# A three-block transformer megakernel on one Trainium2 core: the mixer's decay sums repeated over the partitions by a DMA in place of selector matmuls

## The chip, the core and the metric

The kernel runs on one core of one Trainium2 chip. A core has five engines with queues of their own that work in order and meet in semaphores: TensorE (matmuls, PE in the profile; PEld is its loading of the stationary operand), VectorE (DVE), ScalarE (ACT), GpSimd (POOL) and SyncE (SP), which here issues nearly all DMAs. The metric is the device time of one execution in microseconds. It was 2147.99 us, the median of three runs (2144.83, 2147.99 and 2150.49).

## The reference, cut to what matters

The input is x, 4 batches of 256 rows of 512. Four blocks are added to it one after another: attention, a feed-forward with a row mask, a Mamba-2 mixer, and the feed-forward again. The change is in the mixer, which has 128 heads of 64 channels in 8 groups of 16 heads. With `cum` the running sum of dt times A over the rows of a head, it computes

```python
cum = jnp.cumsum(dA.reshape(b, nc, CS, H), axis=2)
Ldec = jnp.exp(cum[:, :, :, None, :] - cum[:, :, None, :, :])
Ldec = jnp.where(mask[None, None, :, :, None], Ldec, 0.0)
scores = jnp.einsum('bcihn,bcjhn->bcijh', Cc, Bc) * Ldec * dtc[:, :, None, :, :]
y_intra = jnp.einsum('bcijh,bcjhp->bcihp', scores, xc)
...
y = (y_intra + y_inter).reshape(b, l, H, P) + Dp[None, None, :, None] * x
...
g = y * jax.nn.silu(gate)
var = jnp.mean(gg * gg, axis=-1, keepdims=True)
g = (gg * jax.lax.rsqrt(var + EPS)).reshape(b, l, INTER) * norm_w
return g @ out_w.T
```

The reference goes in chunks with a state between them. The kernel computes the same sum in one piece: for every head a full lower triangle of exp(cum_i - cum_j) over the 256 rows of a batch.

## The kernel before

The four blocks run one after another, with a barrier between them. The mixer (`build_mixer`, line 982) takes from about 480 to 2085 us. It starts with a stage of its own for dt and the decay sums (lines 1020 to 1175): DVE computes dt and `cum` as [128 heads, 1024 rows] in fp32, then splits `cum` into three bf16 parts (lines 1132 to 1140), and SP writes each part to DRAM (`cum_parts`, line 1050). TensorE also transposes dt and `cum`, so that rows lie on partitions (`dt_rows`, `ncum_rows`).

Then come 8 groups (`over_groups`, line 1248: the first and the last written out, a loop over the six between), each with 8 pairs of heads, k = 0 to 7. The order on each engine is written out by hand in that engine's `body`. In pair k of group g:

- TensorE (line 1777) makes the two projections for the next pair (x and gate, `product`, 24 matmuls of 512 columns each: fp32 operands are split in a high and a low part, and `three_pass` adds three products), the output products of pairs done before (`out_rows`), and the pair's own y (`y_of_pair`, line 1742: 32 matmuls from `decay` and `x_dt`). `spread_cum` (line 1688) makes the decay sums of one head, one row of 1024 values, stand on all 128 partitions: two matmuls of a constant 0/1 tensor `sel` with `cum`, the group's three bf16 parts, into PSUM banks 2 and 3. It waits until ACT has made the exponentials of the head before (`exped`), since both heads use these banks.
- DVE (line 1595): `causal` takes the minimum of these banks with a mask into `decay` (L1542; a is 0 or 1, the head in the pair); the taps of the convolution (L1518); `mix` multiplies `decay` with the group's C.B product `cb` (L1551); the skip term after y (L1640). In pairs 2 and 3 it adds finished rows to x (L1584).
- ACT (line 1453): `exps` makes 12 exponentials of 128 columns a head, four of them (L1407) straight from banks 2 and 3 and eight in place in `decay` (L1412); between the two heads come the first tap of the convolution, the square, and `scale_wo` (line 1416), which waits for the output weight of this pair, scales it (L1423) and rounds it (L1425); after them the silu functions and `high` (L1434).
- POOL (line 1352): splits of the projection weights (L1308, L1310) and of the output weight (L1323), gating (`gate_pair`, L1333, and g_lo, L1338), sums of squares (L1344).
- SP (line 1279): per pair two loads of projection weights (`load_w`, L1271, each waits for a split three loads back on POOL) and one of the output weight (`load_wo`, L1276, into one of two buffers, waits for the split two pairs back). The weights loaded at pair k of SP's body are those of the projections for pair k+2; the output weight is the one of pair k.

The feed-forward blocks load, after 1 MB of weights, two rows that a DMA repeats over partitions (the cluster numbers over 64, the bias over 128). These are used in the rows below.

Of the kernel before, what the change touches and what calls it, by code (L numbers as in the profile page):

```python
# [15 lines left out]
F32 = mybir.dt.float32  # L16
# [7 lines left out]
P = 128  # L24
# [957 lines left out]
def build_mixer(nc, sh, ins):  # L982
    with ExitStack() as ctx:
# [7 lines left out]
        cum_parts = nc.dram_tensor("cum_parts", (3, MH, ROWS), BF16, kind="Internal").ap()  # L991
# [6 lines left out]
        sel = sb("sel", [3 * GHEADS, GHEADS, P], BF16)  # L998
# [21 lines left out]
        with ExitStack() as inner:  # L1020
            def isb(name, shape, dt=F32):
# [7 lines left out]
            parts = isb("parts", [MH, 3, ROWS], BF16)  # L1029

            made, w_in, c_in, w_done = sem("dt_made"), sem("dt_w_in"), sem("dt_c_in"), sem("dt_w_done")
            proj, step, ex, split, moved = (sem("dt_proj"), sem("dt_step"), sem("dt_exp"), sem("dt_split"),
                                            sem("dt_moved"))
            turned = sem("dt_turned")
            block = inner.enter_context(nc.Block())

            @block.sync
            def _(sp):
# [9 lines left out]
                for part in range(3):  # L1048
                    sp.wait_ge(split, (1, 3, 5)[part])
                    sp.dma_start(cum_parts[part, :, :], parts[:, part, :]).then_inc(moved, 16)  # L1050
                sp.wait_ge(moved, 3 * 16)

            @block.gpsimd
            def _(pool):
# [7 lines left out]
                pool.memset(sel[:, :, :], 0.0).then_inc(made, 1)  # L1062
# [3 lines left out]
                for part in range(3):  # L1066
                    pool.wait_ge(made, 2 + part)
                    pool.affine_select(out=sel[:, :, :], in_=sel[:, :, :], compare_op=ALU.not_equal, fill=1.0,
                                       base=-part * GHEADS, pattern=[[-1, GHEADS], [0, P]], channel_multiplier=1)\
                        .then_inc(made, 1)  # L1070
# [23 lines left out]
            def _(dve):  # L1094
# [32 lines left out]
                dve.wait_ge(made, 2)  # L1127
# [7 lines left out]
                dve.wait_ge(split, 2)  # L1135
                dve.tensor_copy(parts[:, 1, :], e[:, :]).then_inc(split, 1)
                dve.wait_ge(split, 3)
                dve.tensor_tensor(s1[:, :], e[:, :], parts[:, 1, :], ALU.subtract).then_inc(split, 1)
                dve.wait_ge(split, 4)
                dve.tensor_copy(parts[:, 2, :], s1[:, :]).then_inc(split, 1)  # L1140
# [8 lines left out]
            def _(pe):  # L1149
# [17 lines left out]
                STEPS = 17  # L1167
# [16 lines left out]
        cum = sb("cum", [3 * GHEADS, ROWS], BF16)  # L1184
# [15 lines left out]
        cum_arrived = sem("cum_arrived")  # L1200
# [3 lines left out]
        spread, exped, selected, mixed, y_done = (sem("spread"), sem("exped"), sem("selected"), sem("mixed"),  # L1204
                                                  sem("y_done"))
# [60 lines left out]
        def _(sp):  # L1266
# [11 lines left out]

            def body(g, first, last):

                at_least(sp, spread, GHEADS * g)
                for part in range(3):
# [385 lines left out]
        def _(pe):  # L1668
# [19 lines left out]
            def spread_cum(g, k, a, first):  # L1688

                head = GHEADS * g + 2 * k + a  # L1690
                if k == 0 and a == 0:
                    pe.wait_ge(cum_arrived, 3 * 16 * (g + 1))
                    if first:

                        pe.wait_ge(convolved, 12)
# [226 lines left out]
```

## Time and profile before

| | |
|---|---|
| median of the runs | 2147.99 us (2144.83 to 2150.49) |
| profiled execution | span 2145.0 us; the page gives no other time for it |
| PE busy | 1998.4 us, 93% |
| DVE busy | 1469.8 us, 69% |
| ACT busy | 1252.7 us, 58% |
| POOL busy | 1036.5 us, 48% |
| DMA moved | 70.50 MB, mean 33 GB/s |
| granted TensorE clock, mean | 0.957 |

Times in the profile are from the first instruction of the execution. Matmuls overlap, so the duration of one is longer than the step to the next. The timeline merges neighbours of one kind (xcount; the second column is then the time from the first's start to the last's end), and puts the idle time before an instruction, with what ended it, in brackets. The granted clock is 1.00 at 2.4 GHz and 0.50 at 1.2 GHz; in the mixer's loop from 541 to 2056 us it is 1.00 throughout.

### The profile page before, as it was taken

What the parts mean: (1) busy time and instruction counts of PE and PEld (TensorE: products, weight loads), DVE (VectorE), ACT (ScalarE), POOL (GpSimd) and SP (SyncE); (2) the same over time, 40 slices, a digit from 0 to 9 for tenths busy, and PEclk for the clock granted to TensorE, in tenths of its full rate; (3) what the DMA queues carried; (4) which work ended last, traced back from release to release, by engine and by line L of the source; (5) the groups of instructions that cost most, each with busy time, mean ns of one, the idle gap of its engine ahead of it and who ended that gap; (6) DMA issues with size and microseconds to landing.
All of it is one profiled execution on the core that took longest, in us unless ns stands there. A gap on an engine that the chain in (4) does not pass through costs nothing. (4 is left out here: it accounts for less than half of the span.)

```text
span 2145.0 us, 32211 instructions
## 1 busy us (share of the span) xinstructions
PE 1998.4 (93%) x10956; PEld 1533.1 (71%) x10956; DVE 1469.8 (69%) x2060; ACT 1252.7 (58%) x2621; POOL 1036.5 (48%) x841
## 2 busy tenths in 40 slices
PE   6989997758999999999999999999999999999977
PEld 4855775536777777777777777777777777777755
DVE  5466555676677786777768766876777677678756
ACT  3221332326675776667757766775777577666733
POOL 4001001534565566466645654665566466646535
PEclk9965998879999999999999999999999999999988
DMA  3000001001101111110111111111111111111002
GB/s 99 1 1 20 2 2 30 25 27 50 35 30 42 31 40 35 38 35 31 37 37 40 35 37 36 30 40 36 37 35 32 41 31 40 32 40 35 20 1 69
DMA packets 40720, 70.50 MB, mean 33 GB/s; under 512 B 7392, under 2 KB 7520, under 8 KB 40544
## 3 DMA queue, kind: packets, MB, share of 16 engines
q1 hardware_dynamic: 39584, 68.21, 10.5%
q8 instruction: 97, 1.59, 0.3%
q14 instruction: 79, 0.65, 0.1%
q10 hardware_dynamic: 960, 0.05, 0.0%
HBM read 65.34 MB, written 2.88 MB: 32 GB/s over the span
## 5 line engine op out<-in xcount | busy, mean ns | idle before, releaser
L143 PE MATMUL ps<-mix_xnT_hi,mix_w_hi 128*128 128x512 f32 x1152 | 461.8, 401 | 12.0 <-DVE mix_bT L1518 7.0
L145 PE MATMUL ps<-mix_xnT_hi,mix_w_lo 128*128 128x512 f32 x1152 | 455.1, 395 | 0.0
L144 PE MATMUL ps<-mix_xnT_lo,mix_w_hi 128*128 128x512 f32 x1152 | 454.9, 395 | 0.0
L1308 POOL TENSOR_TENSOR mix_w_hi<-mix_w_raw,mix_ones 128x512 fp32r<-128x512 f32 x141 | 178.0, 1263 | 470.0 <-PE ps L145 467.2
L1518 DVE SCALAR_TENSOR_TENSOR mix_xT<-ps,mix_cur,mix_xT 128x510 f32<-128x510 f32 x378 | 280.7, 746 | 108.4 <-ACT mix_xT L1384 99.4
L1412 ACT ACTIVATE mix_decay<-mix_decay,mix_cur_ncum 128x128 f32<-128x128 f32 x1024 | 353.1, 397 | 0.0
L143 PEld LDWEIGHTS ps<-mix_xnT_hi,mix_w_hi 128*128 128x128 f32 x1152 | 217.4, 189 | 63.9 <-issue 12.8
L1551 DVE TENSOR_TENSOR mix_decay<-mix_decay,mix_cb 128x1536 f32<-128x1536 f32 x128 | 242.1, 1897 | 21.8 <-ACT mix_decay L1412 21.2
L145 PEld LDWEIGHTS ps<-mix_xnT_hi,mix_w_lo 128*128 128x128 f32 x1152 | 217.3, 189 | 50.9
L1407 ACT ACTIVATE mix_decay<-ps,mix_cur_ncum 128x128 f32<-128x128 f32 x512 | 183.6, 359 | 117.1 <-DVE mix_decay L1542 117.1
L1333 POOL TENSOR_TENSOR mix_gated<-mix_xT,mix_gated 128x512 f32<-128x512 f32 x128 | 163.8, 1279 | 182.2 <-DVE mix_xT L1640 174.1
L144 PEld LDWEIGHTS ps<-mix_xnT_lo,mix_w_hi 128*128 128x128 f32 x1152 | 217.6, 189 | 47.6
L1434 ACT ACTIVATE mix_g_hi<-mix_gated 128x512 fp32r<-128x512 f32 x128 | 80.9, 632 | 271.2 <-POOL mix_gated L1333 271.2
L143 PE MATMUL ps<-mix_wo_hi,mix_g_hi 128*128 128x512 f32 x512 | 211.4, 413 | 13.2 <-DVE mix_cb L1556 8.6
L1753 PE MATMUL ps<-mix_decay,mix_x_dt 128*64 128x256 f32 x1024 | 205.4, 393 | 5.7 <-issue 5.4
L144 PE MATMUL ps<-mix_wo_lo,mix_g_hi 128*128 128x512 f32 x512 | 203.5, 397 | 0.0
L145 PE MATMUL ps<-mix_wo_hi,mix_g_lo 128*128 128x512 f32 x512 | 203.1, 397 | 0.0
L1640 DVE SCALAR_TENSOR_TENSOR mix_xT<-mix_xT,mix_cur,ps 128x512 f32<-128x512 f32 x128 | 95.6, 747 | 146.1 <-PE ps L1755 146.1
L1310 POOL TENSOR_TENSOR mix_w_lo<-mix_w_raw,mix_w_hi 128x512 fp32r<-128x512 f32 x141 | 181.4, 1287 | 11.1
L1564 DVE TENSOR_TENSOR mix_u<-mix_u,ps 128x512 f32<-128x512 f32 x192 | 126.8, 683 | 75.8 <-PE ps L145 75.7
L1338 POOL TENSOR_TENSOR mix_g_lo<-mix_gated,mix_g_hi 128x512 fp32r<-128x512 f32 x128 | 169.3, 1343 | 0.0
L1542 DVE TENSOR_TENSOR mix_decay<-ps,mask_kq 128x512 f32<-128x512 f32 x256 | 163.9, 682 | 5.1 <-PE ps L1699 3.7
(271 smaller groups left out, 3543.4 us busy)
## 6 DMA issues: line engine op xcount, KB each, us to landing
mix_w_raw<-in_w_in_stream SPq DMA_DIRECT2D x144, 256.0 KB, 2.7
mix_wo_raw<-in_w_out_T SPq DMA_DIRECT2D x64, 256.0 KB, 2.9
att_w_raw<-in_w_attn_T SPq DMA_DIRECT2D x12, 256.0 KB, 2.8
x<-in_x SPq DMA_DIRECT2D x8, 256.0 KB, 5.1
ffn_w_raw<-in_w_ffn_T SPq DMA_DIRECT2D x2, 1024.0 KB, 6.2
out_rows<-x SPq DMA_DIRECT2D x8, 256.0 KB, 2.0
att_wp_raw<-in_w_proj_T SPq DMA_DIRECT2D x4, 256.0 KB, 2.6
cum_parts<-mdt_parts SPq DMA_DIRECT2D x3, 256.0 KB, 2.0
```

Source lines behind the costliest of these rows:

```text
L143: pe.matmul(out, lh, rh, start=(k == 0), stop=False)
L144: pe.matmul(out, lh, rl, start=False, stop=False)
L145: last = pe.matmul(out, ll, rh, start=False, stop=(k == tiles - 1))
L1308: pool.tensor_tensor(w_hi[:, at % 2, :, :], raw, one, ALU.mult).then_inc(w_hi_done, 1)
L1310: pool.tensor_tensor(w_lo[:, at % 2, :, :], raw, w_hi[:, at % 2, :, :].bitcast(F32), ALU.subtract).then_inc(w_lo_done, 1)
L1338: pool.tensor_tensor(g_lo[:, k % 4, cols], gated[:, k % 2, cols], g_hi[:, k % 4, cols].bitcast(F32), ALU.subtract).then_inc(g_lo_done, 1)
L1407: last = act.activation(decay[:, a, b, 2 * P:BLK], ps[:, 2 + b // 2, (b % 2) * T + P:(b % 2 + 1) * T], ACT.Exp, bias=cur_ncum[:, 2 * b, hc ...
L1412: last = act.activation(diag, diag, ACT.Exp, bias=cur_ncum[:, 2 * b + i, hc:hc + 1])
L1518: dve.scalar_tensor_tensor(out=d[:, :, shift:T], in0=src[:, :, 0:T - shift], scalar=w[:, MK - 1 - shift:MK - shift], in1=d[:, :, shift:T], ...
L1542: last = dve.tensor_tensor(decay[:, a, 2 * half:2 * half + 2, 0:T].rearrange("p b (i c) -> p b i c", c=P), ps[:, 2 + half, :].rearrange("p ...
L1551: dve.tensor_tensor(decay[:, a, :, :], decay[:, a, :, :], cb[:, :, :], ALU.mult).then_inc(mixed, 1)
L1753: pe.matmul(out.rearrange("p (a c) -> p a c", c=P), x_dt[:, 2 * b, 64 * a:64 * a + 64], m[:, 0::2, :], start=True, stop=False)
```

## The change

DVE's split in three parts goes, with its three stores. SP writes `cum` once, in fp32, as `cum_rows` (128 heads x 1024). For every head SP then loads the head's row with a broadcast access pattern, 4 KB to each of the 128 partitions, 512 KB in all, into `spread`, which has one buffer for each of the two heads of a pair. The load for a head waits until ACT has made the exponentials of the head two before (`exped`). `spread_cum` and `sel` go; DVE's `causal` and ACT's first exponentials read `spread`.

```diff
-        cum_parts = nc.dram_tensor("cum_parts", (3, MH, ROWS), BF16, kind="Internal").ap()
+        cum_rows = nc.dram_tensor("cum_rows", (MH, ROWS), F32, kind="Internal").ap()
...
-                for part in range(3):
-                    sp.wait_ge(split, (1, 3, 5)[part])
-                    sp.dma_start(cum_parts[part, :, :], parts[:, part, :]).then_inc(moved, 16)
-                sp.wait_ge(moved, 3 * 16)
+                sp.wait_ge(step, STEPS)
+                sp.dma_start(cum_rows, cum[:, :]).then_inc(moved, 16)
+                sp.wait_ge(moved, 16)
...
-                dve.tensor_copy(parts[:, 0, :], cum[:, :]).then_inc(split, 1)
-                dve.wait_ge(split, 1)
-                dve.tensor_tensor(e[:, :], cum[:, :], parts[:, 0, :], ALU.subtract).then_inc(split, 1)
...
+            def load_spread(g, k, a):
+
+                head = GHEADS * g + 2 * k + a
+                at_least(sp, exped, head - 1)
+                sp.dma_start(spread[:, a, :], cum_rows[bass.ds(head, 1), :].broadcast_to([P, ROWS]))\
+                    .then_inc(spread_in[a], 16)
+
             def body(g, first, last):
 
-                at_least(sp, spread, GHEADS * g)
-                for part in range(3):
-                    sp.dma_start(cum[part * GHEADS:(part + 1) * GHEADS, :],
-                                 cum_parts[part, bass.ds(GHEADS * g, GHEADS), :]).then_inc(cum_arrived, 16)
+                if first:
+                    load_spread(g, 0, 0)
+                    load_spread(g, 0, 1)
                 w = ahead(last)
                 for k in range(PAIRS):
-                    for dg, j in w[2 * k:2 * k + 2]:
+                    more = not (last and k == PAIRS - 1)
+                    mine = w[2 * k:2 * k + 2]
+                    for dg, j in mine[:1]:
+                        load_w(LEAD + len(NEXT) * (g + dg) + j, LEAD + j)
+                    if more:
+                        load_spread(g, k + 1, 0)
+                    for dg, j in mine[1:]:
                         load_w(LEAD + len(NEXT) * (g + dg) + j, LEAD + j)
                     load_wo(g, k)
+                    if more:
+                        load_spread(g, k + 1, 1)
...
-                    last = act.activation(decay[:, a, b, 2 * P:BLK],
-                                          ps[:, 2 + b // 2, (b % 2) * T + P:(b % 2 + 1) * T],
+                    last = act.activation(decay[:, a, b, 2 * P:BLK], spread[:, a, b * T + P:(b + 1) * T],
...
-                dve.wait_ge(spread, head + 1)
+                dve.wait_ge(spread_in[a], 16 * (PAIRS * g + k + 1))
...
-                                             ps[:, 2 + half, :].rearrange("p (b i c) -> p b i c", i=2, c=P),
+                                             spread[:, a, half * 512:(half + 1) * 512]
+                                             .rearrange("p (b i c) -> p b i c", i=2, c=P),
...
-            def spread_cum(g, k, a, first):
-
-                head = GHEADS * g + 2 * k + a
-                if k == 0 and a == 0:
-                    pe.wait_ge(cum_arrived, 3 * 16 * (g + 1))
...
-                at_least(pe, exped, head)
-                for half in range(2):
-                    last = pe.matmul(ps[:, 2 + half, :], sel[:, 2 * k + a, :],
-                                     cum[:, half * 512:(half + 1) * 512], start=True, stop=True)
-                last.then_inc(spread, 1)
```

SP's queue in one pair of the loop over groups, before. `mix_w_raw` is a projection weight, `mix_wo_raw` the output weight; an ISA row is the wait ahead of a DMA.

```order
L1271 ISA
L1271 DMA mix_w_raw<-in_w_in_stream 128x512
L1271 ISA
L1271 DMA mix_w_raw<-in_w_in_stream 128x512
L1276 ISA
L1276 DMA mix_wo_raw<-in_w_out_T 128x512
```

The same pair after. `mix_spread` is the buffer of the repeated row, `cum_rows` the sums in DRAM.

```order
L1250 ISA
L1250 DMA mix_w_raw<-in_w_in_stream 128x512
L1262 ISA
L1262 DMA mix_spread<-cum_rows 128x1024
L1250 ISA
L1250 DMA mix_w_raw<-in_w_in_stream 128x512
L1255 ISA
L1255 DMA mix_wo_raw<-in_w_out_T 128x512
L1262 ISA
L1262 DMA mix_spread<-cum_rows 128x1024
```

The first load of `spread` stands between the two loads of projection weights, the second behind the output weight; the second projection weight and the output weight are now queued behind the first one's wait.

TensorE in the loop, from the end of y (L1753, L1755) to the transposes of the next x (L1710), before:

```order
L1753 MATMUL ps<-mix_decay,mix_x_dt 64x256
L1755 MATMUL ps<-mix_decay,mix_x_dt 64x128
L1699 MATMUL ps<-mix_cum,mix_sel 128x512 x2
L1705 REGISTER_ALU
L57 REGISTER_ALU
L1710 MATMUL ps<-ident,mix_xT 128x128 x4
```

and the same place after, where these lines are L1731, L1733 and L1688:

```order
L1731 MATMUL ps<-mix_decay,mix_x_dt 64x256
L1733 MATMUL ps<-mix_decay,mix_x_dt 64x128
L1683 REGISTER_ALU
L57 REGISTER_ALU
L1688 MATMUL ps<-ident,mix_xT 128x128 x4
```

The two selector matmuls are gone and nothing stands in their place. The other place, between the first and the second output product of a pair, loses its two in the same way.

## Rows read from the trace of the kernel before

**Rows 1.** The page, busy us, share of the span, instructions:

```profile
PE 1998.4 (93%) x10956; PEld 1533.1 (71%) x10956; DVE 1469.8 (69%) x2060; ACT 1252.7 (58%) x2621; POOL 1036.5 (48%) x841
```

**Rows 2.** Timeline, TensorE, one pair: start, us, engine, line, operands, [idle before]:

```profile
1004.48 0.65 PE L1753 MATMUL ps<-mix_decay,mix_x_dt 128*64 128x256 f32 x2
...
1008.05 0.60 PE L1699 MATMUL ps<-mix_cum,mix_sel 48*128 48x512 bf16 x2
1008.58 1.09 PE L1710 MATMUL ps<-ident,mix_xT 128*128 128x128 f32 x8
...
1016.57 0.60 PE L1699 MATMUL ps<-mix_cum,mix_sel 48*128 48x512 bf16 x2
1017.11 0.50 PE L143 MATMUL ps<-mix_wo_hi,mix_g_hi 128*128 128x512 f32 x1
...
1027.07 0.65 PE L1753 MATMUL ps<-mix_decay,mix_x_dt 128*64 128x256 f32 x2
```

**Rows 3.** Timeline, ACT, the same pair:

```profile
1014.33 0.70 ACT L1412 ACTIVATE mix_decay<-mix_decay,mix_cur_ncum 128x128 f32<-128x128 f32 x2
...
1016.91 0.71 ACT L1423 ACTIVATE mix_wo_raw<-mix_wo_raw,mix_cur_norm 128x512 f32<-128x512 f32 x1
...
1019.65 0.37 ACT L1407 ACTIVATE mix_decay<-ps,mix_cur_ncum 128x128 f32<-128x128 f32 x1 [1.36 <-DVE mix_decay L1542]
...
1022.43 0.69 ACT L1412 ACTIVATE mix_decay<-mix_decay,mix_cur_ncum 128x128 f32<-128x128 f32 x2
```

**Rows 4.** Timeline, DVE, the same pair:

```profile
1008.82 1.28 DVE L1542 TENSOR_TENSOR mix_decay<-ps,mask_kq 128x512 f32<-128x512 f32 x2
...
1023.15 1.76 DVE L1551 TENSOR_TENSOR mix_decay<-mix_decay,mix_cb 128x1536 f32<-128x1536 f32 x1 [0.16 <-ACT mix_decay L1412]
```

**Rows 5.** Timelines and TensorE's clock, pairs 0 and 1 of the first group:

```profile
516.63 0.65 PE L1753 MATMUL ps<-mix_decay,mix_x_dt 128*64 128x256 f32 x2 [0.27 <-DVE mix_decay L1551]
...
535.29 2.60 DVE L1551 TENSOR_TENSOR mix_decay<-mix_decay,mix_cb 128x1536 f32<-128x1536 f32 x1 [1.86 <-ACT mix_decay L1412]
...
537.99 1.08 PE L1753 MATMUL ps<-mix_decay,mix_x_dt 128*64 128x256 f32 x2 [4.18 <-issue]
...
538.00:539.00 1.00, 1.00 (x3) 0.50 0.38 145
```

**Rows 6.** Timeline, SP, the stores of the three parts:

```profile
472.95 4.25 SPq L1050 DMA_DIRECT2D cum_parts<-mdt_parts  x3
```

**Rows 7.** The page, DMA issues: count, KB each, us to landing:

```profile
mix_wo_raw<-in_w_out_T SPq DMA_DIRECT2D x64, 256.0 KB, 2.9
```

**Rows 8.** Stretches of the first feed-forward's loads; last columns PEclk, DMA share, GB/s:

```profile
370.50:371.00 0.50, 0.50 (x3) 0.50 (x4) 0.19 (x1) 0.46 (x2) 0.40 (x2) 0.50 1.06 393
...
372.75:373.00 0.25, 0.05 (x1) 0.00 (x0) 0.25 (x2) 0.25 (x1) 0.25 (x1) 0.50 1.20 246
```

**Rows 9.** Timeline, POOL, the pair of rows 2:

```profile
1007.63 2.70 POOL L1333 TENSOR_TENSOR mix_gated<-mix_xT,mix_gated 128x512 f32<-128x512 f32 x2 [3.04 <-DVE mix_xT L1640]
```

**Rows 10.** Timelines, DVE and POOL, pair 2 of a group, both reading SBUF:

```profile
1143.51 1.78 DVE L1584 SCALAR_TENSOR_TENSOR x<-mix_u,mix_rstd,x 128x512 f32<-128x512 f32 x1
...
1143.01 1.74 POOL L1338 TENSOR_TENSOR mix_g_lo<-mix_gated,mix_g_hi 128x512 fp32r<-128x512 f32 x1
```

**Rows 11.** Groups of instructions, shapes apart: busy us, mean ns, idle before:

```profile
L1407 ACT ACTIVATE mix_decay<-ps,mix_cur_ncum 128x128 f32<-128x128 f32 x512 | 183.6, 359 | 117.1 <-DVE mix_decay L1542 117.1
L1412 ACT ACTIVATE mix_decay<-mix_decay,mix_cur_ncum 128x128 f32<-128x128 f32 x1024 | 353.1, 397 | 0.0
```

**Rows 12.** Timeline, TensorE, y of pairs 0 and 1 of a group:

```profile
1111.54 0.65 PE L1753 MATMUL ps<-mix_decay,mix_x_dt 128*64 128x256 f32 x2
...
1135.94 0.65 PE L1753 MATMUL ps<-mix_decay,mix_x_dt 128*64 128x256 f32 x2
```

**Rows 13.** Timeline, ACT, pair 0 of that group:

```profile
1099.40 0.70 ACT L1412 ACTIVATE mix_decay<-mix_decay,mix_cur_ncum 128x128 f32<-128x128 f32 x2
```

More of the change, by code:

```diff
@@ L997, in build_mixer @@
         norm_w = sb("norm_w", [P, MG, PAIRS])
-        sel = sb("sel", [3 * GHEADS, GHEADS, P], BF16)
         dt_rows = sb("dt_rows", [P, NT, MH])
@@ L1028, in build_mixer @@
             dt, da, cum, ones = (isb(n, [MH, ROWS]) for n in ("dt", "da", "cum", "ones"))
-            parts = isb("parts", [MH, 3, ROWS], BF16)
             made, w_in, c_in, w_done = sem("dt_made"), sem("dt_w_in"), sem("dt_c_in"), sem("dt_w_done")
-            proj, step, ex, split, moved = (sem("dt_proj"), sem("dt_step"), sem("dt_exp"), sem("dt_split"),
-                                            sem("dt_moved"))
+            proj, step, ex, moved = sem("dt_proj"), sem("dt_step"), sem("dt_exp"), sem("dt_moved")
             turned = sem("dt_turned")
+            STEPS = 17
             block = inner.enter_context(nc.Block())
@@ L1065, in _ @@
                     lead_split(pool, n)
-                for part in range(3):
[L1067 to L1070, printed above, removed]
             @block.scalar
@@ L1126, in _ @@
                 chained(dve.tensor_scalar(da[:, :], dt[:, :], head[:, 2:3], -1.0, ALU.mult, ALU.mult))
-                dve.wait_ge(made, 2)
+                dve.wait_ge(made, 1)
                 for b in range(B):
@@ L1130, in _ @@
                     chained(dve.tensor_tensor_scan(cum[:, tb], ones[:, tb], da[:, tb], 0.0, ALU.mult, ALU.add))
-                dve.tensor_copy(parts[:, 0, :], cum[:, :]).then_inc(split, 1)
-                dve.wait_ge(split, 1)
-                dve.tensor_tensor(e[:, :], cum[:, :], parts[:, 0, :], ALU.subtract).then_inc(split, 1)
[L1135 to L1140, printed above, removed]
                 for n in range(4):
@@ L1183, in build_mixer @@
         bT, cT = sb("bT", [P, ROWS]), sb("cT", [P, ROWS])
-        cum = sb("cum", [3 * GHEADS, ROWS], BF16)
+        spread = sb("spread", [P, 2, ROWS])
         cb = sb("cb", [P, B, BLK])
@@ L1199, in build_mixer @@
         wo_scaled, wo_hi_done, wo_lo_done = sem("wo_scaled"), sem("wo_hi_done"), sem("wo_lo_done")
-        cum_arrived = sem("cum_arrived")
+        spread_in = [sem(f"spread_in{a}") for a in range(2)]
         ones_made, cur_ready = sem("ones_made"), sem("cur_ready")
@@ L1203, in build_mixer @@
         silu_x, silu_g = sem("silu_conv"), sem("silu_gate")
-        spread, exped, selected, mixed, y_done = (sem("spread"), sem("exped"), sem("selected"), sem("mixed"),
-                                                  sem("y_done"))
+        exped, selected, mixed, y_done = sem("exped"), sem("selected"), sem("mixed"), sem("y_done")
         aux, aux_free, u_read = sem("aux"), sem("aux_free"), sem("u_read")
@@ L1782, in body @@
                     if k == 0:
-                        spread_cum(g, k, 0, first)
                         out_with(g, k, (0, 1), first)
@@ L1792, in body @@
                         out_with(g, k, (0,), first)
-                    spread_cum(g, k, 1, first)
                     if k:
@@ L1802, in body @@
                     y_of_pair(g, k, first)
-                    if k < PAIRS - 1:
-                        spread_cum(g, k + 1, 0, first)
                     if has_next and k < PAIRS - 1:
```

5 lines of the change are left out of this document (removed).

## The prediction

> **What bounds the kernel now.** I read the page first: TensorE is busy 93% of the span [rows 1], and that is a share over stages with different limits, so the next view is the timeline of one pair of heads in the mixer's loop, where 64 such pairs make three quarters of the run. The reader is to see there that TensorE starts one matmul after another without a gap, and that a pair lasts 22.59 us, from the first matmul of the pair's y product at 1004.48 to that of the next at 1027.07 [rows 2]. Beside it runs a loop of dependences from y to the next y: DVE adds the skip term, GpSimd gates, ACT copies g_hi and makes the exponentials of head a=0 (last one done at 1014.33 + 0.70), scales the output weight at 1016.91, makes the exponentials of head a=1 (1019.65 to 1023.12) [rows 3], and DVE's mix of that head ends at 1024.91 [rows 4]. TensorE needs it at 1027.07. So TensorE bounds, with 2.2 us between it and the loop. In the first group, where the output products are still missing, the loop bounds: the mix ends at 537.89 and y starts at 537.99 after 4.18 us of idle TensorE [rows 5].
>
> **What it removes.** 256 selector matmuls, two for each of the 128 heads. Their busy sum says little, since matmuls overlap; the slot counts: from the selector's start to the next start 0.53 us after y and 0.54 us between the output products [rows 2], some 1.1 us a pair. With TensorE the only bound that is 64 x 1.1 = 70 us. Before the loop five DVE passes and two of three stores go. The three stores are issued from 472.95 to 477.20 [rows 6]; the one fp32 store can go out when the first of them did, but DVE's copies of dt and the decay sums still follow. I take 3 us saved, between 0 and the 4.25 us of that row. The selector's making on GpSimd ended before the stage and is worth nothing.
>
> **What it moves: SP's queue.** This is the term that decides. SP issues in order. Before, the output weight of pair k was queued behind two weight loads that waited for GpSimd's splits only, and was issued a whole pair ahead of its use. Now the load of `spread` for head (k+1, 0) stands in front of the second weight load and of that output weight, and it waits for `exped`, which ACT signals after the last exponential of head (k, 0). ACT wants the output weight of pair k right after that: it is 1.88 us from the end of the last exponential (1015.03) to the scaling (1016.91) [rows 3], with only a tap and a square between. The three transfers start together, one behind the other: 512 KB of spread, 256 KB, 256 KB. A 256 KB load lands 2.9 us after its issue with nothing ahead of it but one equal load [rows 7]. At the 393 GB/s of an ordinary stream [rows 8] 256 KB are 0.67 us; I take 2.0 us as fixed, since part of the 2.9 is spent behind that equal load. The spread's source is one DRAM row read 128 times. The nearest rows are the feed-forward's bias and cluster numbers, also rows repeated over the partitions: while they are all that is moving, the rate is 246 GB/s [rows 8]. At that, 512 KB take 2.1 us; as an ordinary stream they would take 1.3. From the end of the exponential to the landing: 0.1 for SP, 2.0 fixed, 2.1, 0.67 and 0.67, together 5.5 us. Bounds: 3.4 (the repeated row takes no time of its own) and 6.1 (it takes twice the time of an ordinary stream). By the Trainium skill, DMA: Bandwidth & Descriptors, section Anatomy of one DMA, a transfer takes about 2.0 us and then its bytes at 436 GB/s. By that, 1 MB would be there after 4.4 us as an estimate and a pair be 1.1 us shorter than I make it; the rule is fitted to another issuing path and this trace's repeated rows run slower, so I go by the rows.
>
> **What it adds on DVE, ACT and GpSimd.** The mask step read PSUM and one SBUF tensor; it now reads two SBUF tensors. It starts at 1008.82 [rows 4], in the middle of the two gating steps of GpSimd (1007.63 to 1010.33) [rows 9], and the second of these is on the loop. What two such operations do to each other is seen where DVE adds rows to x beside GpSimd's g_lo: one 128x512 operation of DVE takes 1.78 us, where one of the mask step takes 0.64, and GpSimd's 1.74 us [rows 10], where one gating step takes 1.35; each waits for the other's to end, and they take turns. Here the second gating step would wait for one half of the mask step: 0.5 us; bounds 0 and 1.1 (both halves first). ACT's first exponential of each block reads SBUF for PSUM: 397 against 359 ns [rows 11], four a head, 0.15 us. DVE's time itself I leave as it is. The wait of DVE for `spread_in` costs nothing: the load is issued 15 us before its use.
>
> **The pair after.** From y: 10.55 to the last exponential of head a=0 [rows 2, 3], + 0.15 + 0.5 = 11.2; + 5.5 = 16.7 the output weight is there; + 1.4 scaling and rounding (1016.91 to 1018.29, which is 1019.65 less the 1.36 that the exponential waits) [rows 3]; + 3.47 + 0.15 exponentials; + 1.79 mix [rows 4]; + 0.1 to TensorE [rows 5]: 23.6 us. TensorE alone would need 22.6 - 1.1 = 21.5. The wait takes the place of the selector matmuls and overshoots by 1.0 us a pair. ACT waits 3.6 us for the weight; behind it in ACT's queue stand the exponentials of head a=1, for which DVE's mix and then TensorE wait. The mask step of a=1 and the waits for it (1.36 us before [rows 3]) hide in this.
>
> **Sum.** Pairs 2 to 7 of a group: 6 x 1.02 = 6.1 (23.61 against 22.59). Pair 1 lasts 24.40 us before (1111.54 to 1135.94) [rows 12], with the sums of squares on TensorE; it becomes 23.6: -0.8. Pair 0: its last exponential of head a=0 ends at 1100.10 [rows 13]; + 0.15 + 5.5 + 1.4 + 3.62 + 1.79 + 0.1 gives 1112.66 for 1111.54: +1.1. A group: 6.4, eight groups 51 us. The first group's pair 1 was 21.36 us (516.63 to 537.99) [rows 5], +2.2 in place of -0.8, and its pair 0 some +2; the last pair of all loads nothing ahead and gives back 1: +4. The stage before: -3. Nothing else is touched. 51 + 4 - 3 = 52. The profiled execution's span is 2145.0 us and the page has no other time for it; the median of the runs is 2148.0, 3.0 above. The forecast for the median: 2148 + 52 = 2200 us.
>
> **Rivals.** (a) TensorE stays the bound and the 70 us come: 2148 - 70 - 3 = 2075. It speaks for this that TensorE is 93% busy and nothing else is above 69%. Against it: the loop would have to close in 21.5 us, so the output weight to land 3.4 us after the exponential, or 3.9 if DVE and GpSimd never take turns; with the bound of 3.4 that needs a repeated row that is nearly free. A flaw in my reading of SP's order would give it too. (b) Break-even: the repeated row streams at 393 GB/s (-0.7) and GpSimd and DVE miss each other (-0.5). The pair is 22.4, pairs 1 give -1.2: 50 x -0.15 - 8 x 1.2 - 3 = -20, 2128; with only one of the two it is near 2155 to 2175. (c) Slower still: with the loop bounding, the mix of a=1 falls on GpSimd's weight split, as in the first group, where it took 2.60 for 1.76 us [rows 5], and 0.8 us on 56 pairs are 47 us: 2248. Also the granted clock: after the 4.18 us idle gap in [rows 5] the clock stood at 0.50 (1.2 GHz) in 538 to 539, and two matmuls of y spanned 1.08 us in place of 0.65 [rows 2]. The gap to come is 23.6 - 21.5 = 2.1 us, half of that one, and I expect no fall; if it came in every pair, y would take about 1 us more, 60 us in all.
>
> **How the numbers follow.** Forecast with its own range 2170 to 2230: 0.55. (a): 0.10. (b): 0.17, of which 0.09 faster, 0.05 within 0.3% (6 us, about what a measurement of this kernel can tell from no change) and 0.03 slower. (c): 0.15. The rest, 0.03, a broken transfer far above. Faster 0.19, same 0.06, slower 0.75. The range 2115 to 2250 leaves out (a) and the far part of (c).
>
> **What would show it.** In the changed kernel's profile: in the waits, ACT waiting at the scaling of the output weight for a DMA, 64 times and 3 to 4 us each, which was no wait before; TensorE idle about 2 us before the y product, released by DVE's mix; the pair at 23.6 us; SP waiting for ACT; the mask step of a=0 over 1.28 us for its two halves, and gating over 2.70; the share of the DMA engines up by some 0.1; the granted clock at 1.00 in the loop. A pair near 21.5 us with no DMA wait on ACT would prove the argument on SP's queue wrong; a wait of 2.5 us would prove only the rate of the repeated row too low.

## The result, and the profile after

The changed kernel takes 2258.1 us (median; 2253.5 to 2262.1), the kernel before 2146.5: 1.052 of its time, interval 1.050 to 1.054. That is 112 us more, where I had forecast 52: just above my range, and near rival (c)'s 2248. The profiled executions are 2259.9 and 2145.0 us, 115 apart.

The page after, which answers to [rows 1] and [rows 7]: busy us, share, instructions; then DMA issues with KB each and us to landing.

```profile
PE 1979.3 (88%) x10700; PEld 1556.1 (69%) x10700; DVE 1582.9 (70%) x2055; ACT 1269.3 (56%) x2621; POOL 1122.3 (50%) x837
...
mix_spread<-cum_rows SPq DMA_DIRECT2D x128, 512.0 KB, 4.0
...
mix_wo_raw<-in_w_out_T SPq DMA_DIRECT2D x64, 256.0 KB, 4.3
```

TensorE lost 256 matmuls, but its busy time fell by 19 us only, and DVE and GpSimd gained 113 and 86 us. The waits after (engine and line that waited, what it waited for: us in total, times, longest):

```profile
ACT mix_wo_raw L1415 <- DMA mix_wo_raw<-in_w_out_T: 252.3, 63, 5.5
...
DVE mix_decay L1544 <- ACT mix_decay L1404: 128.5, 64, 6.1
PEld ps L1731 <- DVE mix_decay L1544: 108.3, 49, 4.6
```

They form the predicted chain: ACT waits for the output weight, 4.0 us on average, DVE's mix waits for ACT, TensorE's y for the mix. Two groups of instructions before (busy us, mean ns, idle before), then the same two and the gating after:

```profile
L1753 PE MATMUL ps<-mix_decay,mix_x_dt 128*64 128x256 f32 x1024 | 205.4, 393 | 5.7 <-issue 5.4
...
L1542 DVE TENSOR_TENSOR mix_decay<-ps,mask_kq 128x512 f32<-128x512 f32 x256 | 163.9, 682 | 5.1 <-PE ps L1699 3.7
```

```profile
L1731 PE MATMUL ps<-mix_decay,mix_x_dt 128*64 128x256 f32 x1024 | 241.2, 458 | 120.5 <-DVE mix_decay L1544 87.0
...
L1326 POOL TENSOR_TENSOR mix_gated<-mix_xT,mix_gated 128x512 f32<-128x512 f32 x128 | 181.8, 1420 | 273.4 <-DVE mix_xT L1633 266.7
...
L1534 DVE TENSOR_TENSOR mix_decay<-mix_spread,mask_kq 128x512 f32<-128x512 f32 x256 | 270.8, 1098 | 1.4 <-DVE mix_cur_ncum L1596 1.3
```

One half of the mask step (L1534) went from 682 ns to 1098 in the mean. The y matmuls went from 393 ns to 458, although nothing in them changed: the granted clock, shown below, is what changed. One steady pair on TensorE, two starts of y, which answer to 1004.48 and 1027.07 of [rows 2]:

```profile
1064.83 0.65 PE L1731 MATMUL ps<-mix_decay,mix_x_dt 128*64 128x256 f32 x2 [2.94 <-DVE mix_decay L1544]
...
1090.82 0.69 PE L1731 MATMUL ps<-mix_decay,mix_x_dt 128*64 128x256 f32 x1 [2.96 <-DVE mix_decay L1544]
```

The pair is 25.99 us, after 2.94 us of idle TensorE. Stretches of it follow (us; PE, PEld, DVE, ACT and POOL busy; PEclk, DMA share, GB/s):

```profile
1066.00:1067.00 1.00, 1.00 (x10) 0.86 (x8) 0.00 (x0) 0.99 (x2) 0.00 (x0) 0.50 0.30 104
...
1070.90:1071.90 1.00, 1.00 (x7) 0.83 (x6) 1.00 (x2) 0.00 (x0) 0.88 (x1) 1.00 0.00 0
```

PEclk stands at 0.50 (1.2 GHz) a microsecond after the gap and is back at 1.00 when y is over. y takes 5.3 us and not 3.6. Over all 64 pairs, y was this slow (over 4 us) behind 25 of the 31 gaps of 2.9 us or more, and behind 1 of the 33 shorter ones. Then SP, ACT, DVE and GpSimd in the same pair, which answer to [rows 3, 4, 9]:

```profile
1077.67 0.33 SPq L1262 DMA_DIRECT2D mix_spread<-cum_rows  x1
1078.19 0.33 SPq L1250 DMA_DIRECT2D mix_w_raw<-in_w_in_stream  x1
1078.72 0.33 SPq L1255 DMA_DIRECT2D mix_wo_raw<-in_w_out_T  x1
```

```profile
1076.82 0.68 ACT L1404 ACTIVATE mix_decay<-mix_decay,mix_cur_ncum 128x128 f32<-128x128 f32 x2
...
1083.44 0.72 ACT L1415 ACTIVATE mix_wo_raw<-mix_wo_raw,mix_cur_norm 128x512 f32<-128x512 f32 x1 [4.33 <-DMA mix_wo_raw<-in_w_out_T]
...
1084.73 0.39 ACT L1400 ACTIVATE mix_decay<-mix_spread,mix_cur_ncum 128x128 f32<-128x128 f32 x1
...
1087.66 0.68 ACT L1404 ACTIVATE mix_decay<-mix_decay,mix_cur_ncum 128x128 f32<-128x128 f32 x2
```

```profile
1070.79 2.38 DVE L1534 TENSOR_TENSOR mix_decay<-mix_spread,mask_kq 128x512 f32<-128x512 f32 x2
...
1088.37 2.39 DVE L1544 TENSOR_TENSOR mix_decay<-mix_decay,mix_cb 128x1536 f32<-128x1536 f32 x1 [2.72 <-ACT mix_decay L1404]
```

```profile
1071.02 1.61 POOL L1326 TENSOR_TENSOR mix_gated<-mix_xT,mix_gated 128x512 f32<-128x512 f32 x1 [0.86 <-DVE mix_xT L1633]
...
1086.77 1.04 POOL L1301 TENSOR_TENSOR mix_w_hi<-mix_w_raw,mix_ones 128x512 fp32r<-128x512 f32 x1
1087.88 1.26 POOL L1303 TENSOR_TENSOR mix_w_lo<-mix_w_raw,mix_w_hi 128x512 fp32r<-128x512 f32 x1
```

0.2 us after the last exponential of head a=0, SP issues the three loads it held back. The weight is usable 5.9 us after that exponential. The last mix then meets GpSimd's split (L1303) and takes 2.39 us, not 1.76.

### The profile page after: what moved, and what is told of

Its sections match the earlier page's. It is cut to its first block and busy times, and to the rows that moved or that the text cites. A ratio compares the mean times of both kernels' runs of the same rounds, so it can differ in the third digit from the quotient of the medians.

```text
span 2259.9 us, 31926 instructions
## 1 busy us (share of the span) xinstructions
PE 1979.3 (88%) x10700; PEld 1556.1 (69%) x10700; DVE 1582.9 (70%) x2055; ACT 1269.3 (56%) x2621; POOL 1122.3 (50%) x837
## 5 line engine op out<-in xcount | busy, mean ns | idle before, releaser
L1731 PE MATMUL ps<-mix_decay,mix_x_dt 128*64 128x256 f32 x1024 | 241.2, 458 | 120.5 <-DVE mix_decay L1544 87.0
L1544 DVE TENSOR_TENSOR mix_decay<-mix_decay,mix_cb 128x1536 f32<-128x1536 f32 x128 | 256.3, 2002 | 128.5 <-ACT mix_decay L1404 128.5
L1326 POOL TENSOR_TENSOR mix_gated<-mix_xT,mix_gated 128x512 f32<-128x512 f32 x128 | 181.8, 1420 | 273.4 <-DVE mix_xT L1633 266.7
L1534 DVE TENSOR_TENSOR mix_decay<-mix_spread,mask_kq 128x512 f32<-128x512 f32 x256 | 270.8, 1098 | 1.4 <-DVE mix_cur_ncum L1596 1.3
L1301 POOL TENSOR_TENSOR mix_w_hi<-mix_w_raw,mix_ones 128x512 fp32r<-128x512 f32 x141 | 165.8, 1176 | 210.4 <-PE ps L145 207.6
L1303 POOL TENSOR_TENSOR mix_w_lo<-mix_w_raw,mix_w_hi 128x512 fp32r<-128x512 f32 x141 | 220.9, 1567 | 11.0
L143 PE MATMUL ps<-mix_wo_hi,mix_g_hi 128*128 128x512 f32 x512 | 205.7, 402 | 23.5 <-DVE mix_cb L1549 12.3
L1316 POOL TENSOR_TENSOR mix_wo_lo<-mix_wo_raw,mix_wo_hi 128x512 fp32r<-128x512 f32 x64 | 114.1, 1783 | 192.0 <-ACT mix_wo_hi L1417 192.0
L1400 ACT ACTIVATE mix_decay<-mix_spread,mix_cur_ncum 128x128 f32<-128x128 f32 x512 | 199.9, 390 | 12.5 <-DVE mix_decay L1534 11.9
L1731 PEld LDWEIGHTS ps<-mix_decay,mix_x_dt 128*64 128x64 f32 x1024 | 101.7, 158 | 147.7 <-DVE mix_decay L1544 108.3
```

The source lines that it names most:

```text
L143: pe.matmul(out, lh, rh, start=(k == 0), stop=False)
L1301: pool.tensor_tensor(w_hi[:, at % 2, :, :], raw, one, ALU.mult).then_inc(w_hi_done, 1)
L1303: pool.tensor_tensor(w_lo[:, at % 2, :, :], raw, w_hi[:, at % 2, :, :].bitcast(F32), ALU.subtract).then_inc(w_lo_done, 1)
L1326: pool.tensor_tensor(gated[:, k % 2, cols], xT[:, k % 2, cols], gated[:, k % 2, cols], ALU.mult)\
L1400: last = act.activation(decay[:, a, b, 2 * P:BLK], spread[:, a, b * T + P:(b + 1) * T], ACT.Exp, bias=cur_ncum[:, 2 * b, hc:hc + 1])
L1534: last = dve.tensor_tensor(decay[:, a, 2 * half:2 * half + 2, 0:T].rearrange("p b (i c) -> p b i c", c=P), spread[:, a, half * 512:(half + ...
```

## The experiments

The recorded expectations use three names. Theory 1 is the output weight's place in SP's queue, behind a load that waits; rival 1 is the traffic of the repeated rows itself; rival 2 is that DVE and GpSimd take turns. Each line of this table is a steady pair late in a group, read from the timelines from the start of y, in us; where the pairs of a kernel differ much, its line gives their range:

```
kernel                    y     last exp a=0   to scaling   last mix   pair    slow y's
before                   3.63      10.55          1.9         1.76     22.59     1
changed, clock up        3.63      11.06          5.6         2.67     24.33    26
  clock down             5.26      12.67          5.9         2.39     25.99
weight first             3.63      11.05          1.5         1.76     22.9      1
8 fillers                3.63      11.05          5.6         2.7      24.36     2
4 fillers             3.6 to 5.3  11.0 to 12.7  5.5 to 7.7  1.8 to 2.9  24.3 to 27.1  16
mask in PSUM             3.63      10.70          5.7         1.8      23.1      7
both                     3.63      10.71          1.5         1.76     21.32     2
before, loads in place 3.6 to 5.3 10.5 to 12.2  5.6 to 7.5  1.8 to 2.8  22.7 to 25.7  5
before, loads behind     3.63      10.54          1.9         1.76     22.59     1
zeros, one row           3.63      11.05          5.5         2.76     24.32    22
zeros, distinct rows     3.63      11.05          4.8         2.0      22.9      3
zeros, quarter           3.63      11.05          5.1         1.8      23.0      3
```

"To scaling" runs from the end of that exponential to the scaling of the output weight. "Slow y's" counts the pairs, of 64, whose y lasted over 4 us; in the two lines of the changed kernel it is one count.

**The output weight ahead of the waiting loads.**

```diff
-                    for dg, j in mine[:1]:
-                        load_w(...)
-                    if more:
-                        load_spread(g, k + 1, 0)
-                    for dg, j in mine[1:]:
+                    for dg, j in mine:
                         load_w(...)
                     load_wo(g, k)
                     if more:
+                        load_spread(g, k + 1, 0)
                         load_spread(g, k + 1, 1)
```

> The changed kernel with one reordering on SP: each pair's output weight is issued ahead of the two repeated-row loads of the next pair, not between them. Nothing else moves; the same transfers are made. Theory 1 (the output weight stands behind a load that waits for the pair's exps, and that is the main cost): ScalarE's waits for the output weight, 252 us in all, go nearly to nothing; the chain of a pair (12.7 us to the last exp of the first head, 1.3 for the weight's scaling, 3.6 of exps, 2.4 of mix, 0.1) is then 20.1 us, below TensorE's own 21.5, TensorE's idle before y falls from about 3 us to under 0.5, its clock stays at 1.0 in the loop, and the kernel takes about 2085 us (2065 to 2110), faster than the kernel before the change. Rival 1 (the 64 MB of repeated rows themselves slow the other work or the other loads): the wait moves to another transfer or the engines stay slow, 2190 to 2260. Rival 2 (mask step and gating taking turns on two SBUF operands is what costs): the chain stays late, 2140 to 2180.

2165.0 us, 1.008 of the kernel before (1.006 to 1.010): 93 us better than the changed kernel, but not 173. The wait for the weight is gone, as theory 1 said, and the loop still does not close below 22.9 us. What stands there now is the mask step of head a=1, in DVE's, GpSimd's and ACT's timelines:

```profile
1066.31 1.73 DVE L1531 TENSOR_TENSOR mix_decay<-mix_spread,mask_kq 128x512 f32<-128x512 f32 x1
...
1067.95 1.78 DVE L1531 TENSOR_TENSOR mix_decay<-mix_spread,mask_kq 128x512 f32<-128x512 f32 x1
```

```profile
1065.07 2.42 POOL L1334 TENSOR_TENSOR mix_squares<-mix_squares,mix_square 128x1024 f32<-128x1024 f32 x1
1067.43 1.75 POOL L1313 TENSOR_TENSOR mix_wo_lo<-mix_wo_raw,mix_wo_hi 128x512 fp32r<-128x512 f32 x1
```

```profile
1069.77 0.41 ACT L1397 ACTIVATE mix_decay<-mix_spread,mix_cur_ncum 128x128 f32<-128x128 f32 x1 [3.50 <-DVE mix_decay L1531]
```

DVE's first half ends 0.55 us after GpSimd's squares (1067.49), the split 1.1 us after that half, the second half 0.55 us after the split. Each of them alone takes about that long, so each waited for the one before: 3.42 us for two halves, against 1.28 before, and the exponentials of a=1 wait 3.50 us. My theory had left this second cost out of the loop, because in the changed kernel the wait for the weight covers it.

**TensorE kept busy in the gap.** Eight matmuls whose result nobody reads stand ahead of each y.

```diff
+                for j in range(8):
+                    pe.matmul(ps[:, 2 + j % 2, :], xnT_hi[:, 0, 0:P], xnT_hi[:, 0, 0:512], start=True, stop=True)
                 at_least(pe, y_skip, 2 * pair)
```

> The changed kernel with 8 matmuls of 512 columns more per pair on TensorE, into two PSUM banks that the changed kernel leaves free, right ahead of the pair's y, where TensorE now waits about 3 us; their result is not used. Theory 1 with the clock fall as its second part: at full clock they take about 1.8 us and fit into the wait, the clock no longer falls to 0.5, the y of a pair takes 3.6 us and not 5.2, and the chain that starts from its end is 1 to 1.6 us shorter in each of about 50 pairs: 2175 to 2215 us, though TensorE does 15 us of work per 8 pairs more. If the clock fall costs nothing of its own (the wait for the weight alone sets the pair, y ends early enough either way), the time stays at 2250 to 2275. Rival 1 (traffic) and rival 2 (turns of VectorE and GpSimd) expect no gain either.

2246.5 us, 1.047 (1.045 to 1.050): 12 us better. The clock part came true; the whole did not. The y group after it, to be read against 241.2 us and 458 ns of the changed kernel, and the start of a pair:

```profile
L1733 PE MATMUL ps<-mix_decay,mix_x_dt 128*64 128x256 f32 x1024 | 207.6, 398 | 36.9 <-DVE mix_decay L1544 25.2
```

```profile
1056.38 0.65 PE L1733 MATMUL ps<-mix_decay,mix_x_dt 128*64 128x256 f32 x2 [1.12 <-DVE mix_decay L1544]
```

Slow y's fell from 26 to 2 and the pairs late in a group to 24.4 us (changed kernel: 24.3 to 27.2). But pairs 1 to 3 of a group, which had almost no gap, went from 23.4 to 23.6 up to 25.1: 1.5 x 3 x 7 = some 32 us given back. From the first y to the last are 63 pairs; added over those of the changed kernel, y is 47.5 us longer than 3.63 each, and that is the clock's share there. 47.5 less 32 is near the 12 us measured.

**Four fillers and not eight** (range(4) in the same diff).

> The changed kernel with 4 matmuls of 512 columns ahead of each pair's y, not 8: 0.93 us at full clock, so they fit where the wait is 2 us too. With 8, y took 3.63 us in every pair looked at (5.0 to 6.5 without them) and those pairs 24.36 us and not 25.7 to 27.1, but the whole gained 12 us only, since the fillers cost up to 1.9 us in pairs that do not wait so long. Theory 1: if the clock stays up with 4 as well, the gain is 20 to 45 us: 2215 to 2240. If 4 are too few, y stays at 5 us in those pairs and the time at 2250 to 2265.

2264.7 us, 1.055 (1.053 to 1.057): no gain, a miss. 16 y's stayed slow, pairs 1 to 3 still took 24.2 to 24.8, and the wait for the output weight grew from 252 to 281 us:

```profile
ACT mix_wo_raw L1415 <- DMA mix_wo_raw<-in_w_out_T: 281.2, 63, 6.0
```

The trace shows what the later weights have in common: a 16 KB transfer of instructions on the same DMA engines. In the kernel with four fillers it falls between issue and landing of 34 of 62 output weights (all but the first and the last), which land after 5.3 us in the mean; the other 28 land after 4.4. All 22 that took over 5.0 us are among the 34. In the changed kernel it hit only 3 of the 62. 0.9 x 34 = 31 us is about the growth of the wait, 29. One such load, from its kernel's DMA view of that stretch:

```profile
q8 instruction: 1, 0.02, 1.0%
...
mix_wo_raw<-in_w_out_T SPq DMA_DIRECT2D x1, 256.0 KB, 6.0
```

That the transfer of instructions delays the load is inferred from this; no run sets it apart, and why its times fell otherwise is open.

**The mask read from PSUM.** One matmul of the identity with the mask fills a free bank; DVE waits for it once.

```diff
-                                             sh.mask_kq[:, :].unsqueeze(1).unsqueeze(1).broadcast_to([P, 2, 2, P]),
+                                             ps[:, 3, 0:P].unsqueeze(1).unsqueeze(1).broadcast_to([P, 2, 2, P]),
...
+            pe.matmul(ps[:, 3, 0:P], sh.ident16[:, :], sh.mask_kq[:, :], start=True, stop=True).then_inc(mask_made, 1)
```

> The changed kernel with the constant causal mask read by VectorE's mask step from a free PSUM bank, where one matmul puts it at the start, and not from SBUF: the step then reads one SBUF operand and one PSUM operand, as it did before the change. The wait for the output weight stays. Theory 1: this takes 1.0 us of the 2.4 us that two mask steps take now, some tenths of GpSimd's gating beside them, and so 1.0 to 1.4 us of a pair's chain; 60 to 80 us over the kernel, 2180 to 2200. Rival 2 (these turns are the main cost): the whole excess over the kernel before goes, 2140 to 2165. Rival 1 (traffic): VectorE's steps are slow from the transfers' writes, 2245 to 2265, the mask step still over 1000 ns.

2181.4 us, 1.017 (1.015 to 1.019): 77 us better, as expected. The mask step is what it was, 163.5 us in all:

```profile
L1537 DVE TENSOR_TENSOR mix_decay<-mix_spread,ps 128x512 f32<-128x512 f32 x256 | 163.5, 680 | 1.4 <-DVE mix_cur_ncum L1599 1.3
```

Only 0.35 us of it is on the stretch to the last exponential (11.05 to 10.70). The larger part is the last mix, which no longer meets the split (1.8 for 2.7), and 19 slow y's fewer.

**Both edits.**

> Both edits together: the output weight issued first, and the mask in PSUM. Theory 1: with the weight's wait gone TensorE sets the pair at 21.5 us, so the shorter mask step adds little: 0 to 15 us better than the reordering alone, 2060 to 2095. Rival 1: 2180 to 2250. Rival 2: clearly better than the reordering alone, by 60 us or more.

2076.6 us, 0.967 of the kernel before (0.966 to 0.969): 182 us better than the changed kernel and 69 better than the one before. A steady pair is 21.32 us and TensorE is bound again:

```profile
PE 1924.4 (93%) x10701; PEld 1523.4 (73%) x10701; DVE 1445.6 (70%) x2055; ACT 1267.2 (61%) x2621; POOL 1071.4 (52%) x837
...
L1731 PE MATMUL ps<-mix_decay,mix_x_dt 128*64 128x256 f32 x1024 | 207.5, 398 | 13.0 <-issue 10.0
```

The second edit is worth 88 us on top of the first, where I had expected 15 at most. So rival 2's condition held as well: each of the two waits alone keeps the loop above TensorE's time.

**Place in the queue against traffic.** The kernel before, whole, with the repeated-row loads beside it, in the changed kernel's places and into one buffer that nobody reads.

```diff
+                sp.dma_start(spread_t[:, :], cum_rows[bass.ds(head, 1), :].broadcast_to([P, ROWS]))\
+                    .then_inc(spread_in, 16)
```

> The kernel before the change, whole, with its selector matmuls; beside them the fp32 rows go to DRAM and SP issues the changed kernel's repeated-row loads, in the changed kernel's places and behind the same waits, into a buffer that nobody reads (one of 4 KB where the changed kernel has two, so each load also waits for the one before it). This is the position in SP's queue and the traffic, without the change's new operands. Theory 1, from the rows: from y to the last exp of the first head 10.55 us as before, then 5.6 to the scaling, 4.9 to the last exp, 1.8 to 2.7 of mix: 22.9 to 23.7 us a pair against 22.59; with pair 0 and the clock's falls 2160 to 2200 us. If the waits cost nothing without the slower mask step (the pair stays TensorE-bound) 2145 to 2155. If the traffic itself is what costs, VectorE and GpSimd slow down here as well: over 2200.

2219.1 us, 1.033 (1.031 to 1.035): more than expected. ACT waited 249.1 us, 60 times, for the output weight, as in the changed kernel; DVE's mask step stayed at 682 ns and its mix at 1894. Late in the groups the weight was usable 5.6 to 7.5 us after the exponential, where I had put 5.6. The long ones go with the same transfer of instructions: it falls on 48 of the 62 output weights, which land 5.0 us after issue in the mean against 4.4 for the others, and on all 26 that took over 5.0. So up to 0.55 x 48 = 26 us of this kernel's excess is that coincidence and not the queue's place.

The next kernel is the same with one difference: the output weight is issued ahead of the loads that wait.

> As the run with the loads alone (the kernel before, with repeated-row loads that nobody reads), but the output weight is issued ahead of the loads that wait for the exps. What is left is the traffic: 64 MB more through the DMA engines, in the same stretches. Theory 1 (place in the queue, not traffic): the wait for the output weight is gone, a pair takes 22.59 us as before, and the time is that of the kernel before within 0.5%, 2142 to 2157 us. Rival 1 (traffic): it stays at 2190 or more.

2147.6 us, 1.0005 (0.9995 to 1.0015), with 22.6 us a pair. The loads take as long to land as anywhere:

```profile
mix_spread_t<-cum_rows SPq DMA_DIRECT2D x128, 512.0 KB, 4.3
mix_w_raw<-in_w_in_stream SPq DMA_DIRECT2D x144, 256.0 KB, 4.6
mix_wo_raw<-in_w_out_T SPq DMA_DIRECT2D x64, 256.0 KB, 4.8
```

64 MB more of traffic cost nothing that can be measured. The same loads, put ahead of the output weight and not behind it, cost 71 us more, up to 26 of them by the coincidence above.

**What of the wait is bytes.** Three kernels whose decay sums in DRAM are zeros, so that it doesn't matter for the values which row or how much of it is read. They leave out the decay, and their results are not the reference's. The base, with one row repeated as in the changed kernel:

```diff
-                sp.dma_start(cum_rows, cum[:, :]).then_inc(moved, 16)
+                sp.dma_start(cum_rows, low[:, :]).then_inc(moved, 16)
...
+                pool.memset(low[:, :], 0.0).then_inc(made, 1)
```

> The changed kernel on other numbers: the rows in DRAM are zeros (a tile that GpSimd clears, 1 us more in the stage before), and the bias of the exps is zero, so the decay is 1 left of the diagonal. Same transfers, same instructions, same order. It is the base for the next two. All theories: 2250 to 2265 us, as the changed kernel (2258).

On that base, 128 different rows:

```diff
-                sp.dma_start(spread[:, a, :], cum_rows[bass.ds(head, 1), :].broadcast_to([P, ROWS]))\
+                sp.dma_start(spread[:, a, :], cum_rows[:, :])\
```

> As the kernel with zeros, but each transfer reads 128 different rows of DRAM (all zeros as well) in place of one row 128 times; the same 512 KB arrive at the same time, the decay sums used are not the head's own. If reading one row 128 times is what makes the transfer slow (246 GB/s in the changed kernel's stretches against 393 GB/s for a plain load, rows of before), each of the 512 KB transfers is about 0.8 us shorter, ScalarE's wait for the output weight goes from 4.3 to 3.5 us in each pair, and the kernel takes 2195 to 2215 us. If the repeated read is no slower than a plain one, the wait and the time stay, 2250 to 2265.

And on the base, the first quarter of the one row:

```diff
+                cols = ROWS if whole else ROWS // 4
+                sp.dma_start(spread[:, a, 0:cols], cum_rows[bass.ds(head, 1), 0:cols].broadcast_to([P, cols]))\
```

> As the kernel with zeros, but each transfer of the loop brings only the first quarter of the row (128 KB), so most of the decay row is an older one. Queue order and waits are the same. Theory 1: the output weight still stands behind a transfer that waits for the exps, but that one is 1.6 us shorter (2.1 at 246 GB/s to 0.5); the fixed part of the wait (about 3.5 us: issue, 2 us of latency, the two weights) stays. A pair is 1.6 us shorter: 24.35 to 22.8, and with less waiting the clock falls in fewer pairs: 2140 to 2175 us. Rival 1 (the traffic itself, 64 MB, slows the engines or all loads) expects at least as much, and the mask step faster than 1098 ns. Were it the position in the queue alone, and not the bytes, the time would stay at 2235 or more.

The base took 2249.2 us (1.046; 1.043 to 1.050), the distinct rows 2175.3 and the quarter 2176.0 (both 1.013; 1.011 to 1.015). The distinct rows gained 20 us more than I had expected at most, the quarter 1 us less than at least. DMA issues of the distinct rows, then of the quarter:

```profile
mix_spread<-cum_rows SPq DMA_DIRECT2D x128, 512.0 KB, 3.2
```

```profile
mix_spread<-cum_rows SPq DMA_DIRECT2D x126, 128.0 KB, 3.5
```

And one stretch of each in which that load is under way: changed kernel, distinct rows, quarter (columns as above, the last is GB/s):

```profile
1079.00:1080.40 1.40, 1.40 (x8) 1.15 (x7) 1.36 (x2) 0.12 (x1) 1.40 (x2) 1.00 0.77 268
```

```profile
1044.20:1045.40 1.20, 1.20 (x7) 0.99 (x6) 1.13 (x2) 0.16 (x1) 1.20 (x2) 1.00 0.92 364
```

```profile
1075.40:1076.80 1.40, 1.40 (x8) 1.14 (x7) 1.33 (x3) 0.27 (x1) 1.40 (x2) 1.00 0.36 91
```

The rates I had taken from [rows 8] are near these: 268 GB/s against 246 for one row, 364 against 393 for many. These are stretches in the middle of a load. 512 KB of distinct rows land 0.7 us earlier than the 3.9 of one row, as worked out. By the Trainium skill, DMA: Bandwidth & Descriptors, section Anatomy of one DMA, 512 KB take about 3.2 us as an estimate, by a rule fitted to loads that GpSimd issues: the distinct rows take 3.2, one row repeated 3.9. A quarter of the bytes saved 0.4 us, not 1.6: at 1 KB a piece the row comes at 91 GB/s. Both are 128 pieces, so here the pieces set the time more than the bytes.

Yet each of these small gains was worth 73 or 74 us. Since the weight came 0.4 to 0.7 us earlier, the last mix got clear of GpSimd's split (2.76 to 2.0 and 1.8 us), and with the shorter gap the slow y's fell from 22 to 3. With the distinct rows the 63 pairs are 71 us shorter: 35 by y, 14 by the last mixes, 22 by the rest. The loop pays three times for one late load.

**The selector's making put back** on GpSimd, unused:

```diff
+                for part in range(3):
+                    pool.wait_ge(made, 2 + part)
+                    pool.affine_select(out=sel[:, :, :], in_=sel[:, :, :], ...).then_inc(made, 1)
```

> The changed kernel with the making of the selector put back on GpSimd in the stage before (one clear, three selects, with their waits); nobody reads it. I forecast this to be worth nothing; the trace has the scan end 3.6 us earlier without it, since VectorE's steps on two SBUF operands beside the three selects are no longer slowed. If that is right, the scan ends at 472 us of the span again and not at 468.5, VectorE's three steps there take 2.4 to 2.9 us again, and the time is 2 to 5 us over the changed kernel's, about 2262. If it is worth nothing, the scan's end stays at 468.5.

2255.1 us, 1.049 (1.046 to 1.052): not the 2262 expected, and in the whole not to be told from the changed kernel, but plain in DVE's timeline. With the selects, then in the changed kernel:

```profile
452.43 2.55 DVE L1113 TENSOR_TENSOR mdt_s<-mdt_s,mdt_e 128x1024 f32<-128x1024 f32 x1
455.01 2.91 DVE L1114 TENSOR_TENSOR mdt_w<-mdt_s 128x1024 f32<-128x1024 f32 x1
...
469.96 2.87 DVE L1128 TENSOR_TENSOR_SCAN mdt_cum<-mdt_ones,mdt_da 128x256 f32<-128x256 f32 x4
```

```profile
452.81 1.23 DVE L1106 TENSOR_TENSOR mdt_s<-mdt_s,mdt_e 128x1024 f32<-128x1024 f32 x1
454.07 1.22 DVE L1107 TENSOR_TENSOR mdt_w<-mdt_s 128x1024 f32<-128x1024 f32 x1
...
465.66 2.87 DVE L1121 TENSOR_TENSOR_SCAN mdt_cum<-mdt_ones,mdt_da 128x256 f32<-128x256 f32 x4
```

The scan ends at 472.83 against 468.53. The three steps beside the selects take 4.7 us longer with them, 7.84 us (2.55, 2.91 and 2.38) against 3.14.

## Why the prediction was wrong in size and right in kind

The steps, against a pair of the changed kernel at full clock:

- **SP's queue** (5.5 us to the landing): 5.6 at full clock, 5.9 in the slow pair shown. 63 waits of 4.0 us where I had written 64 of 3 to 4. Right, and shown to be place and not traffic by the two runs on the kernel before.
- **To the last exponential** (11.2): 11.06; of the 0.5 us that I gave the turns, 0.35 came (the run with the mask in PSUM). Scaling and exponentials of a=1 (1.4 + 3.62 = 5.0): 4.9. Right.
- **Pair 2 at +1.02, pair 1 at -0.8, pair 0 at +1.1:** of the changes that no slow y disturbs, pairs 2 and 3 are at +1.0, pair 1 at -1.0 and pair 0 at +0.4 to +1.3. Right.
- **The last mix at 1.79 us** is the first step that failed. In pairs 4 to 7 it meets GpSimd's split of the next weight and takes 2.2 to 2.8; with y at full clock those pairs are at +1.7. I had this as half of rival (c) and gave it 0.8 us on 56 pairs. It came as 0.5 to 1.0 on 26 of the 32 such pairs: over the 63 pairs the last mixes are 22 us longer than before.
- **"The gap to come is 2.1 us, and I expect no fall"** is the step that cost most. With the mix late the gap was 2.9 us, and in 25 of 63 pairs y was slow, in all but one of them behind such a gap or a longer one; the y's were 47.5 us longer in sum. In the whole loop the clock was 0.96, where I had written 1.00. I had bounded the fall at 60 us, from the one gap of 4.18 us in the rows, and then put it at nothing; no row showed that a gap of 2.1 us is harmless. The two errors are one: I priced the gap from a pair that was too short.
- **"The selector's making ... is worth nothing"** was wrong by 4.7 us at the scan: the selects ran beside three of DVE's steps, from 451.19 to 459.08 in the kernel before, and slowed them. The loop starts at 473.2 and not at 479.5, 6.3 us earlier, where I had said 3; by the first y 3.1 of it are left (513.48 for 516.63). That is no evidence for the 3: in the variants of the changed kernel that leave this stage's work as it is, the first y starts anywhere from 507.9 to 512.5.
- **"DVE's time itself I leave as it is"**: two halves of the mask step went from 1.28 to 2.38 us. On the path to the first exponentials only 0.35 us of it counts, but in the reordered kernel the second mask step takes 3.42 us and bounds the loop. A cost behind a larger wait looks free until that wait goes.

The sum of measured changes: over the 63 pairs +116 us, before the first y -3.1, in the last y, itself slow, and behind it +1.8; together 115 of 115. Of the 116, 46 are y's clock (47.5 less 1.6 in the kernel before) and 22 the last mixes. The other 48 answer to the steps that I had priced at 55 for the loop. (The 4 of these for the two ends should have been 3: the first group's pair 0 is in the eight groups already.) So the mechanism was right; the two terms that came with the wait were too small, one put at nothing and one left to a rival.

Rival (a)'s 2075 us was a real time of this design: without the queue's wait and with the mask out of SBUF it takes 2076.6, and the pair 21.32 where I had put TensorE alone at 21.5. Rival (b) did not happen. Rival (c) was the nearest, at 0.15: I had its parts and gave them too little, since they follow from the very wait I forecast.

## What to carry over

A load that must wait for a late event holds back every load behind it in its queue: put it behind those that are ready, and count that before the bytes. When a wait opens on the path, price its companions with it (the clock after the gap, the next operation pushed onto a neighbour's), since they come and go together. Before removing an operand from PSUM, look who else reads SBUF at that time; the two edits together turned 5% slower into 3% faster.

## What the runs showed of the hardware

- A DVE operation on two SBUF operands and a GpSimd operation take turns: a mask step of two halves beside GpSimd's took 1.28, 2.38 and 3.42 us with none, one and two GpSimd operations in its way. With one operand in PSUM it stayed at 1.28, and so did GpSimd's gating at 1.28 us (1.42 in the changed kernel).
- It holds for a select of GpSimd too: DVE's 128x1024 step on two SBUF operands 2.55 against 1.23 us.
- One DRAM row read 128 times: 268 GB/s at 4 KB a partition, 91 GB/s at 1 KB; 128 different rows 364 GB/s, each in the middle of one load.
- A 256 KB load with a 16 KB transfer of instructions under way landed after 5.3 us against 4.4 (four fillers), 5.0 against 4.4 (loads in place). Shown is that they go together.
- Behind gaps of 2.9 us or more TensorE's granted clock was down to 1.2 GHz in 25 of 31 pairs of the changed kernel, behind shorter ones in 1 of 33; in the kernels whose pairs took 22.9 to 23.1 us it was so in 1 to 7 pairs.
